# Attention in groups of 512 queries instead of 256, with the weighted sum laid between the next group's scores

## What is computed

```
def ffn(x):                       # I = 704, weights and inputs rounded to blocks of fp4
    gate, y = q(x) @ q(w_gate).T, q(x) @ q(w_up).T
    return q(silu(gate) * y) @ q(w_down).T
def attn(x):                      # one head of width 2 x 256, 2048 keys for each query
    q, k, v = x @ Wq.T + bq, x @ Wk.T + bk, x @ Wv.T + bv
    w = softmax(q @ k.T / 16)
    return (w @ v) @ Wo.T + bo
x = x + 0.5 * ffn(layernorm(x))
x = x + attn(layernorm(x))
x = x + 0.5 * ffn(layernorm(x))
```

## Time and profile before

| | |
|---|---|
| median of 3 runs | 966.46 us |
| profiled execution | 967.06 us |
| its span | 965.2 us (1.86 us lie around it) |
| PE busy | 923.0 us, 96% |
| DVE busy | 709.6 us, 74% |
| ACT busy | 656.5 us, 68% |
| POOL busy | 506.6 us, 52% |

### The profile page before, as it was taken

The page is one execution under the profiler, slowest core; times in us unless marked ns, Lnnn a source line. Parts: engine busy times, 40 slices in busy tenths (PEclk is TensorE's granted clock), DMA queues, the critical chain, the costliest instruction groups (busy, mean ns, idle before and its releaser), DMA issues.

```text
span 965.2 us, 18233 instructions
## 1 busy us (share of the span) xinstructions
PE 923.0 (96%) x6607; PEld 864.7 (90%) x6607; DVE 709.6 (74%) x1180; ACT 656.5 (68%) x1380; POOL 506.6 (52%) x593
## 2 busy tenths in 40 slices
PE   3889999999989999999999999999989999999997
PEld 2678888889889899999999999999988888989896
DVE  7888988997747755666565545555577899999996
ACT  4767788888765676666657666666685756666653
POOL 3455666666530364444555544444483565656552
PEclk9899999999999999999999999999999999999999
DMA  9100000000000000000000000000000000000001
GB/s 318 40 1 1 1 1 1 2 1 1 1 1 2 1 2 2 1 2 2 1 2 1 1 2 1 2 1 1 2 1 1 1 23 23 22 23 23 23 1 44
DMA packets 11560, 13.94 MB, mean 14 GB/s; under 512 B 848, under 2 KB 10576, under 8 KB 11472
## 3 DMA queue, kind: packets, MB, share of 16 engines
q1 hardware_dynamic: 11472, 12.79, 4.0%
HBM read 8.59 MB, written 4.19 MB: 13 GB/s over the span
## 4 chain that ended last, share of the span: by engine, by line
PE 83%; DVE 8%; ACT 5%; issue 3%; DMA 1%; POOL 1%; SPq 0%; DVEq 0%; ACTq 0%
PE bank L1516 22%; PE bank L1747 18%; PE bank L1419 7%; PE bank_b L1527 6%; PE bank_b L1534 4%; PE bank_b L1799 3%; PE bank_b L1795 3%; PE bank L1795 3%; PE bank_b L1797 3%; PE bank L1799 3%; PE bank L1797 3%; PE bank L1702 2%; PE bank L1555 2%; DVE rounded L700 1%; PE bank_b L1722 1%
## 5 line engine op out<-in xcount | busy, mean ns | idle before, releaser
L530 POOL TENSOR_TENSOR p_lo<-s_buf,p_hi 128x512 fp32r<-128x512 f32 x128 | 165.2, 1296 | 210.1 <-ACT p_hi L1318 198.9
L492 POOL TENSOR_TENSOR zq<-grid,s_neg 128x64 f32<-128x64 f32 (+2 forms) x188 | 177.2, 966 | 48.6 <-DVE grid L706 47.0
L1516 PE MATMUL bank<-w_hi,T_hi 128*128 128x512 f32 (+1 forms) x384 | 149.8, 390 | 5.3 <-DVE z L667 3.1
L1747 PE MATMUL bank<-q_hi,k_hi 128*128 128x256 f32 x512 | 145.2, 284 | 0.1
L1747 PE MATMUL bank<-q_lo,k_hi 128*128 128x256 f32 x512 | 144.9, 283 | 0.0
L1747 PE MATMUL bank<-q_hi,k_lo 128*128 128x256 f32 x512 | 144.8, 283 | 0.0
L1516 PE MATMUL bank<-w_hi,T_lo 128*128 128x512 f32 (+1 forms) x384 | 144.3, 376 | 0.0
L1516 PE MATMUL bank<-w_lo,T_hi 128*128 128x512 f32 (+1 forms) x384 | 144.2, 375 | 0.0
L1303 ACT ACTIVATE s_buf<-bank 128x512 f32<-128x512 f32 x128 | 76.3, 597 | 96.2 <-PE bank L1747 96.2
L1154 ACT ACTIVATE T_hi<-bank 128x1024 fp32r<-128x1024 f32 (+1 forms) x72 | 68.8, 956 | 93.0 <-PE bank L1419 92.9
L859 DVE TENSOR_TENSOR top<-bank,top 128x512 f32<-128x512 f32 x96 | 66.4, 692 | 65.8 <-ACT s_buf L1303 65.7
(11 more groups left out here) (206 smaller groups left out, 2530.1 us busy)
## 6 DMA issues: line engine op xcount, KB each, us to landing
out<-x SPq DMA_DIRECT2D x7, 512.0 KB, 3.1
x<-in_L_attn_hidden_states SPq DMA_DIRECT2D x3, 1024.0 KB, 13.9
x<-in_L_attn_hidden_states SPq DMA_DIRECT2D x2, 512.0 KB, 8.1
wraw<-in_L_ffn_w_down SPq DMA_DIRECT2D x1, 704.0 KB, 9.0
wraw<-in_L_ffn_w_gate SPq DMA_DIRECT2D x1, 640.0 KB, 4.6
wraw<-in_L_ffn_w_up SPq DMA_DIRECT2D x1, 640.0 KB, 6.8
wq_s<-in_L_attn_Wq SPq DMA_DIRECT2D x1, 512.0 KB, 8.3
wk_s<-in_L_attn_Wk SPq DMA_DIRECT2D x1, 512.0 KB, 9.6
```

The source lines that it names most:

```text
L492: last = nc.gpsimd.tensor_tensor(out=blocks(zq[:, to:to + hi - lo]), in0=blocks(grid[:, lo:hi]), in1=spread(s_neg[:, par, lo // BLOCK:hi / ...
L530: nc.gpsimd.tensor_tensor(out=p_lo[:, n % 2, 2 * c:2 * c + 2, :], in0=score_buf(n, c), in1=p_hi[:, 2 * c:2 * c + 2, :].bitcast(F32), op=AL ...
L1516: last = nc.tensor.matmul(gu[:, lo:hi], lhsT=T[:, par, HK + kd, :], rhs=w[:, kd, lo:hi], start=n == 0, stop=n == len(terms) - 1)
L1747: last = nc.tensor.matmul(score_bank(c)[:, a, :], lhsT=kk[:, kd, t], rhs=q[:, n % 2, kd, :], start=i == 0 and a == 0, stop=i == len(terms) ...
```

## The change

QT becomes 4: a group has 512 queries, there are 4 groups a batch and 8 in all. A chunk is now one key tile (CH = 16), so that a score tile is still 128 x 512 and fills one bank. A score chunk is 6 matmuls with 512 moving columns, into one of two banks instead of four. A group's weighted sum needs four output banks, which it holds from its first chunk to `finish`. Score tiles and `p_lo` lie in a ring of RING = 22 slots, `p_hi` in a ring of PR = 4. PE runs `weighted_values(n - 1, c - 2)` right behind `scores(n, c)` (c - 4 in the last group), and ACT's, DVE's and POOL's orders are rewritten to match.

```
-    QT = 2
+    QT = 4
-    CH = NS // 2
+    CH = NS
+    RING = CH + 6
+    PR = 4
 def score_bank(c):
-            return bank4[:, c % 4, :].rearrange("p (a q) -> p a q", q=QT * P)
+            return bank5[:, c % 2, :]
 def scores(n, c):
+                if c >= 2:
+                    pe.wait_ge(evac_done, CH * n + c - 1)
+                if c >= 3:
+                    pe.wait_ge(top_done, tops(n, c - 2))
+                t = slice(c * P, (c + 1) * P)
...
+                    last = nc.tensor.matmul(score_bank(c), lhsT=kk[:, kd, t], rhs=q[:, kd, :], ...)
 def weighted_values(n, c):
+                for a in range(QT):
+                    if c == 0 and n:
+                        pe.wait_ge(x_att, QT * (n - 1) + a + 1)
 def p_upper(n, c):                                  # ACT
+                if g >= PR:
+                    act.wait_ge(pv_done, g - PR + 1)
 def evacuate(n, c):                                 # ACT
+                if g >= RING:
+                    act.wait_ge(pv_done, g - RING + 1)
 # PE
             for n in range(1, NQ):
+                if n == HQ:
+                    for c in range(7):
+                        weighted_values(n - 1, c)
+                        if c in (0, 2, 4):
+                            pe.wait_ge(klo_done, NG + c // 2 + 1)
+                            pe.wait_ge(qlo_done, KD * (n + 1))
+                            transpose_keys(1, c // 2 + 1)
+                    for c in range(9):
+                        scores(n, c)
+                        weighted_values(n - 1, c + 7)
...
+                lag = 4 if n == NQ - 1 else 2
+                for c in range(CH):
+                    scores(n, c)
+                    if c == 0 and n % HQ != 1:
+                        weighted_values(n - 2, CH - 1)
+                    if lag <= c < CH - 1:
+                        weighted_values(n - 1, c - lag)
...
+                elif n + 1 < NQ:
+                    queries(n + 1)
+                    transpose_top(n)
+                    weighted_values(n - 1, CH - 3)
+                    spread_shift(n)
+                    weighted_values(n - 1, CH - 2)
             n = NQ - 1
+            weighted_values(n - 1, CH - 5)
+            transpose_top(n)
+            weighted_values(n - 1, CH - 4)
+            weighted_values(n - 1, CH - 3)
+            spread_shift(n)
+            weighted_values(n - 1, CH - 2)
+            transpose_chain(1, -4)
+            weighted_values(n - 1, CH - 1)
+            chain_lower(1, -4, 0)
+            weighted_values(n, 0)
+            weighted_values(n, 1)
+            pe.wait_ge(lo_done, number_lo(1, -4))
+            transpose_chain(1, -3)
+            weighted_values(n, 2)
+            weighted_values(n, 3)
+            chain_lower(1, -3, 1)
+            for c in range(4, 7):
+                weighted_values(n, c)
+            pe.wait_ge(diff_done, CH * NQ)
+            for columns in range(3):
+                gate_up(0, columns)
+            pe.wait_ge(lo_done, number_lo(1, -3))
+            transpose_chain(1, -2)
+            weighted_values(n, 7)
...
 # DVE, n == HQ
+                    maximum(n - 1)
+                    shift_of(n - 1)
+                    keys_lower(1, 0)
+                    shifted(n - 1, 0)
+                    finish(n - 2)
+                    queries_lower(n, 0)
+                    queries_lower(n, 1)
+                    shifted(n - 1, 1)
+                    shifted(n - 1, 2)
+                    keys_normalised(2)
+                    keys_lower(1, 1)
...
```

More of the change, by code:

```diff
@@ L944, in _ @@
-            shifted(0, CH - 1)
-            maximum(1)
-            shift_of(1)
-            queries_lower(2)
-            for c in range(CH):
-                shifted(1, c)
-            for n in range(2, NQ):
-                b = n // HQ
-                finish(n - 2)
+            for c in range(7, 13):
+                running_top(0, c)
+                row_term(3 + c)
+            row_terms_whole(0)
+            running_top(0, 13)
+            running_top(0, 14)
+            running_top(0, 15)
@@ new lines, in _ @@
+            for n in range(1, NQ):
+                if n == HQ:
+                    maximum(n - 1)
[9 more added lines that the diff above has]
+                    keys_lower(1, 1)
+                    shifted(n - 1, 3)
+                    shifted(n - 1, 4)
+                    keys_normalised(3)
+                    keys_lower(1, 2)
+                    shifted(n - 1, 5)
+                    shifted(n - 1, 6)
+                    keys_lower(1, 3)
+                    for c in range(7, CH):
+                        shifted(n - 1, c)
+                        running_top(n, c - 7)
+                    finish(n - 1)
+                    running_top(n, 9)
+                    running_top(n, 10)
+                    for c in range(11, CH):
+                        values_lower(1, c - 11)
+                        running_top(n, c)
+                    values_lower(1, 5)
+                    continue
+                queries_lower(n, 0)
+                maximum(n - 1)
+                shift_of(n - 1)
+                queries_lower(n, 1)
+                if n % HQ == 1:
+                    values_lower(n // HQ, 6)
+                    values_lower(n // HQ, 7)
+                shifted(n - 1, 0)
+                shifted(n - 1, 1)
+                if n >= 2 and n != HQ + 1:
+                    finish(n - 2)
@@ L979, in _ @@
-                if n == 6:
-                    row_terms_whole(1)
+                    if c + 2 < CH:
+                        shifted(n - 1, c + 2)
+                    if n in (1, 2) and c % 2:
+                        row_term(NS * 3 // 2 - VH * (2 - n) + c // 2)
+                if n == 2:
+                    row_terms_whole(1)
+            n = NQ - 1
+            maximum(n)
+            shift_of(n)
+            scales(-4, 0)
+            scaled(-4)
+            shifted(n, 0)
             to_grid(-4)
-            finish(NQ - 2)
+            shifted(n, 1)
@@ L983, in _ @@
             scales(-3, 1)
             scaled(-3)
+            finish(n - 1)
+            for c in range(2, 5):
+                shifted(n, c)
             second_blocks(-4, 0)
+            for c in range(5, CH):
+                shifted(n, c)
             second_blocks(-3, 1)
@@ L1396, in _ @@
-                if n == HQ - 1:
-                    new_statistics(n - 2)
+                    if n == 1 and c in (4, 7):
+                        statistics(NT - 2 + (c - 4) // 3, NT - 2 + (c - 4) // 3)
+                    if n >= 2 and c in (4, 7, 10, 13):
+                        new_statistics(QT * (n - 2) + (c - 4) // 3)
+            n = NQ - 1
+            normalise(0)
+            absolute(-4)
+            normalise(1)
+            for c in range(2):
+                exponential(n, c)
+                p_upper(n, c)
@@ L1398, in _ @@
+            chain_upper(-4, 0)
             absolute(-3)
             normalise(2)
+            for c in range(2, 4):
+                exponential(n, c)
+                p_upper(n, c)
             chain_rest(-4, 0)
-            nc.scalar.activation(warm[:], mhalf[:, 0:1], ACT.Silu)
+            exponential(n, 4)
             absolute(-2)
             normalise(3)
-            silu_gate(0)
-            chain_upper(-3, 1)
-            chain_rest(-3, 1)
-            normalise(4)
-            new_statistics(NQ - 2)
@@ L1409, in _ @@
-            ffn_rounds(step2, -2)
+            chain_upper(-3, 1)
+            p_upper(n, 4)
+            exponential(n, 5)
+            p_upper(n, 5)
+            chain_rest(-3, 1)
+            for c in range(6, 11):
+                exponential(n, c)
+                p_upper(n, c)
+            for c in range(11, CH):
+                exponential(n, c)
+            nc.scalar.activation(warm[:], mhalf[:, 0:1], ACT.Silu)
+            silu_gate(0)
+            p_upper(n, 11)
+            absolute(-1)
```

561 lines of the change are left out of this document (249 added, 312 removed).

## The result

| | before | after |
|---|---|---|
| median | 966.72 us (965.96 to 967.00, 4 runs) | 989.19 us (987.39 to 991.35, 4 runs) |
| profiled execution, its span | 967.06, 965.2 us | 987.39, 985.6 us |
| PE busy | 923.0 us | 922.1 us |
| PE's mean granted clock | 0.993 | 0.984 |

A forecast was written before the change was run, and what follows sets the result against it. PE, never idle inside attention, was taken as the bound. Its work -13.5, group ends and starts +0.8 +1.2 +1.7, batch's change +12.9, last group +9.4: +12.5 us on 967.06, 979.6, so 979; range 960 to 989.

The forecast's parts named there:

- PE's work in steady state: Attention on PE: wider score and query matmuls and fewer transposes save 13.5 us; two old groups' 50.6 become about 49.1.
- The starts of the first groups of each batch: PE waits 2.0 us at the first batch's start, as much as before, and 1.2 in batch 1, where nothing was lost.
- four other group ends: Steady-state ends of groups, where PE turns to the next group: 0.2 us of waiting each, 0.8 in all.
- the 1.7 in the last group: Last group, lag 4: scores 1 to 4 follow each other with no sum between, behind `finish`; 1.7 us.
- The first p tile and the key blocks: Batch's change: PE waits 2.4 us for the second p tile, then 2.4 twice and 0.6 once at later key blocks.
- The last group's waits: PE waits from the end of the last scores on: 14.5 us in sum, 9.4 more than the 5.1 before.
- the rest: Last group: `finish` before ffn round 0 costs 1.3 us and DVE's lateness in round 1 costs 0.9.
- Scores and sums in alternation: Batch's change, eight steps: p tile waits for the evacuation, 2.3 us; statistics lengthen four steps by 0.75 each, 3.0.
- the first: Rival: exposed waits stay covered and only PE's work changes, 953.5 us, to 958 with group starts; chance 0.16.
- The third: Rival: last group worse, DVE's small operations and POOL's lower parts slow each other on SBUF, 986 us; chance 0.20.
- The second: Rival: either the batch's change or the last group is mostly hidden, 970 or 966 us; chance 0.17.
- The rule about wide matmuls: Scores on PE: one 512-column matmul replacing two of 256 gains 1.9 us by the skill's rule, 7.7 by the rows.

The follow-up runs named there:

- e11: Changed kernel with only group 4's four new_statistics on ACT moved behind the alternation of scores and weighted sums: 988.63 us, ratio 1.0230.
- e12: Changed kernel with only DVE's shifted and ACT's exponential and p_upper one p tile ahead in group 4, statistics unmoved: 981.43 us, ratio 1.0147.
- e9: On top of e6 and e7 together, more instruction orders changed on DVE, POOL and ACT, no work added or removed: 962.66 us, ratio 0.9956.
- e6: Changed kernel reordered at the batch's change: key blocks later, one p tile ahead, statistics later, first p tiles earlier: 976.37 us, ratio 1.0101.
- e7: Changed kernel reordered in the last group: add_bias early, ACT's last evacuation ahead of group 6's last exponential and p_upper: 981.73 us, ratio 1.0154.
- e3: Changed kernel with DVE and ACT one p tile ahead in group 4's alternation and the four new_statistics moved behind it: 981.73 us, ratio 1.0155.
- e5: Changed kernel with dummy matmuls of 512 columns, results unread, put inside five of PE's waits: 983.10 us, ratio 1.0161.
- e10: e6 and e7 together plus dummy matmuls, 9 ahead of group 3's weighted chunk 3 and 6 ahead of chain -2: 968.25 us, ratio 1.0018.

## Why the prediction was right in sign and too small

Right, with the size:
- PE's work in steady state: two groups of before against one of now, 50.6 to about 49.1 forecast, 50.6 to 48.75 measured; no idle time there. (The weighted sum has 1536 matmuls and not 3072, half of what the prediction writes; it is the same before and after, so its sum does not change.)
- The starts of the first groups of each batch: PE waits 1.15 twice (2.3 in all by the list of waits), against 2.0 and 1.2 forecast. Of the 0.8 at four other group ends nothing is there, and of the 1.7 in the last group, with no sum between its scores, 0.95; one wait of 0.54 for `finish` ahead of the value blocks was not listed. Together 1.9 too much.
- The first p tile and the key blocks: 2.4, 2.4 and 2.4 forecast, with 0.6 more for a fourth; 2.35, 2.21 and 2.23 measured, and the fourth is not there. 1.0 too much.
- The last group's waits, forecast and measured: top 2.1 and 1.99; chain -4 0.9 and 0.83; `finish` 1.5 and 1.55; lower part of chain -4 1.7 and 1.33; p tiles 1.6 and 0.87; chain -2 4.5 and 4.58; the rest 2.2 and 1.4 (0.69 and 0.72). Together 14.5 and 12.6, and one of 0.75 for chain -1 that was not listed: 1.2 too much.

Wrong:
- **Scores and sums in alternation.** The prediction had the p tile start 0.5 us behind the evacuation's start, and so steps of 3.1 us, with the statistics as a second cause that lengthens four of them to 3.85. In fact the exponential waits for a `shifted` that stands behind `running_top` on DVE, and starts 1.95 us behind the evacuation's start. With that the prediction's own formula gives (0.2 + 1.95 + 2.7 + 2.81) / 2 = 3.83 a step, with statistics or without; measured are 3.93. The eight steps took 30.9 us where 27.8 (four of 3.1, four of 3.85) were forecast, 3.1 more. The statistics cost nothing, which `e11` shows, and the order costs all of it, which `e12` shows. The step looked at ACT's queue and not at DVE's, one engine up the chain.
- **The clock.** Every wait was priced at its own length. About 5.9 us of slower matmuls behind them were in no term; filling the waits gave 6.1 back.

So 12.5 forecast + 3.1 + 5.9 - 1.9 - 1.0 - 1.2 = 17.4, against 987.39 - 967.06 = 20.3 between the profiled executions. The 2.9 that are missing are shown by no row one by one. The waits above are idle times, and idle time is less than what the starts show as lost, as in the eight steps; and the prediction took off 5.1 us for the last group of before, counted by starts, where its idle time is 4.0. The medians lie 22.5 apart, mostly since this profiled execution was the fastest of its four.

Of the rivals, the first (all waits stay covered, 953.5) fell at once, though its direction is real: with other orders `e9` reaches 962.7. The third came out at the right height, 986, for the wrong reason. POOL's lower parts next to DVE's small operations did not grow: the mean of all 128 is 1.30 us before and now, and the 1.18 of the earlier trace rows was a share of the chain, low for one of them. The four `grid` operations between 700 and 750 us took 0.42 or 0.43 us each, none of them the 1.40 of the earlier trace rows (another operation of these chains, `y`, took 1.27 and 1.18, where it had 0.74 and 1.20 before), and the last group's waits came out shorter than forecast, not longer. The second, that one of the two places is mostly hidden, fell too: `e6` gives back 12.8 at the one and `e7` 7.5 at the other. The rule about wide matmuls, 1.9 us by the Trainium skill ("TensorE: Matmul & The Clock Gate", Back-to-back issue gap) and 7.7 by the rows, is decided for the rows as far as it goes: halves cost 0.79 us a group in steady state, 6.3 over eight, and the whole kernel 4.1.

## What to carry to other kernels

When work that was ready a whole stage ahead becomes work that is made just in time, walk the chain of one tile through every engine's queue, and at each instruction ask what stands directly ahead of it and what that waits for; the longest such loop sets the period, and other work that fits in its gap is free, as the statistics were here. Then move only those instructions: here orders alone took the changed kernel from 989.2 to 962.7. Price a wait of about 2 us on a busy PE above its length, since the matmuls behind it may run at the lower clock, as they did behind the 1.99 us here, and look at the granted clock in short windows, because a mean of 0.984 against 0.993 hides it.

## What the runs showed of the hardware

- A PE that had worked at a granted clock of 1.00 since 495 us fell to the lower level after a wait of 1.99 us (from 706.3 us on), and again after one of 4.58 us. Not each such wait does it: behind the waits of 2.21 and 2.23 us at 496 and 502 us it stayed up (the windows below), while in `e3` and `e12`, behind waits of the same length there (2.22 and 2.23), the window from 495 to 500 us has 0.66.

```profile
500.00:505.00 5.00, 2.77 (x20) 2.40 (x19) 2.40 (x3) 2.36 (x4) 2.56 (x2) 1.00 0.00 0
505.00:510.00 5.00, 4.58 (x30) 3.88 (x29) 0.91 (x2) 2.35 (x4) 1.28 (x1) 1.00 0.00 0
```

- In `e9`, with waits of up to 1.54 us in attention, it fell in no window there in the profiled execution, and five executions lie within 1.7 us; the changed kernel's four spread over 4.0 us, at mean clocks from 0.981 to 0.986.
- Matmuls whose result nobody reads, placed inside long waits, took less time than they gave back (6.1 us net, in `e5`); in `e10` that could not be seen again.
- In pairs with a weight load each, fp32r matmuls start 0.12 us apart at 256 columns and 0.23 at 512.
